# A gated cross-attention and expert block: input norm and attention in one part, context first

## The chip, the cores and the metric

The kernel runs on one NeuronCore of a Trainium2 chip. The engines are TensorE (PE; its weight loads are shown as PEld), VectorE (DVE), ScalarE (ACT), GpSimd (POOL) and the queue of SyncE (SP), which starts the DMAs. Each engine works through its own list of instructions in order and waits on semaphores. The metric is the device time of one execution in microseconds; lower is better.

## The reference

`x` is 8 sequences of 112 tokens with 512 channels (896 tokens), the context 8 sequences of 375 rows. The part around the change is this, cut to what matters:

```python
ln_out = _ln(hidden_states, ln_w, ln_b)          # hidden_states is a layer norm of x
q  = _ln(fp8_linear(ln_out, wq,  q_in_scale))    # 16 heads of 128
qx = _ln(fp8_linear(ln_out, wqx, qx_in_scale))
k  = _ln(fp8_linear(ln_out, wk,  k_in_scale))    # 8 groups
v  = fp8_linear(ln_out, wv, v_in_scale)
core = _gqa(q, k, v)
kx, vx = jnp.split(cond @ w_kv_x.T, 2, axis=-1)
xout = _gqa(qx, _ln(kx), vx)
catq = _div_clamp_fp8(concatenate([core, xout]), proj_smooth)
out  = catq @ wproj.T * (proj_in_scale * proj_w_scale)
```

`fp8_linear` divides its input by a scale, clips it to 448, rounds it to eight-bit floating point and multiplies it with the weights. The result goes through a tanh gate, is added to x, and a second part follows with another norm and eight experts of which each token takes two. That second part is not touched.

## The kernel before, in words

The kernel is written for five engines with every wait by hand. It has three parts, each a block of its own.

`quantise_inputs` (lines 231 to 400) is the input norm. The 896 tokens lie as TJ = 7 tiles of 128 in `xs`. Each tile is normed twice, one norm behind the other (the list NORMS, lines 238 to 244): DVE's bn_stats and bn_aggr (373, 363 to 366), GpSimd's power and product (303, 305), ACT's scaling in place (314). PE turns the tiles (347), ACT copies them with the norm's weight and bias into `hT` (320) and scales them once for each of the four projections into `yq` (330). DVE rounds each of the four, 3584 columns at a time, with five operations that wait for one another (`round_fp8`, 410 to 414), into `xq`. Between these, the weights of the first group (4 blocks k of 128 x 2048) are centred per head: DVE takes the means (130, 133), ACT applies them (149 to 154).

`attention` (472 to 1205) goes over 4 groups of heads, and in each over 8 sequences. `passes` (543 to 555) gives the order for all engines: first a step for (0,0) that only projects, then `step(s, t, ...)` in which the projections of s and the attention of t, the one before it, are interleaved. A position s = (g, u) with u < 7 has a tile of tokens. The six projections of a position (`project`, 852 to 877) are: 0 queries, 1 cross queries, 2 keys and values, 3 to 5 the three chunks of the context. They use the two banks of `p_proj` in turn, so that `project` j waits until ACT's `take` (709) of j - 2 is done. Their weights exist as a high and a low part (`w_hi` by ACT, 684; `w_lo` by DVE or GpSimd, 567), as does the context (`c_hi` by ACT, 689; `c_lo` by GpSimd, 638). Before a position's first projection DVE casts its tile of `xq` (`inputs`, 1043 to 1050).

In a step DVE's list is: `sums(s, 0)`, `max_self`, `max_cross` 0 and 1, `norm_self` (1080), `norm_cross` 0 and 1 (1093), `take_self` (1099), and so on, then `smoothed` 0 and 1 (1111) with `inputs` of the next position between them, in the first four steps of a group `weights.means` for the next group, and the rounding of the results (`results.exponents`, `results.rounded`, 196 to 215). PE's list (979 to 1010) has `project(s, 3)` between the scores and `turn_self` (926), which needs norm_self. For the first position, `first`, ACT makes all of w_hi, then c_hi, then takes 0 to 5 (823 to 829); DVE makes w_lo of three pieces (1190 to 1202) and GpSimd of two (647 to 649).

SP loads x, the small vectors and the weights in `quantise_inputs` (279 to 289) and the context of the first sequences in `attention`.

`projected_experts` (from 1212) is the output projection and the experts.

Of the kernel before, what the change touches and what calls it, by code (L numbers as in the profile page):

```python
# [19 lines left out]
U16 = mybir.dt.uint16  # L20
# [40 lines left out]
def transformer_block(nc, x, ctxT, vecs, scalars, smooth, w_in, wproj, Wr, Wg, Wu, Wd, out):  # L61
# [3 lines left out]
    with ExitStack() as top:  # L65
# [24 lines left out]
        with ExitStack() as c:  # L90
            xq = sb(c, "xq", [P, 4, KB, NT], BF16)
            smi = sb(c, "smi", [P, GP, 8])
            wsc = sb(c, "wsc", [P, 4, KB])
            wmul = sb(c, "wmul", [P, KB, LNC // HD])
            weights = CentredWeights(c, sb, sem, w_in, shared, wsc, wmul)
            with ExitStack() as c0:
                quantise_inputs(nc, c0, sb, ps, sem, x, vecs, scalars, smooth, vec, scal, gate,
                                proj_scale, ident, mhalf, epst, xq, smi, weights)
            with ExitStack() as c1:
                attention(nc, c1, sb, ps, sem, ctxT, wproj, cat_w, vec, ident, mhalf, epst, xq, smi,  # L100
                          weights, shared, wp_load, cat_load, results)
# [5 lines left out]
class CentredWeights:  # L107
# [3 lines left out]
    def __init__(self, c, sb, sem, w_in, shared, wsc, wmul):  # L111
# [3 lines left out]
        self.in_done = sem(c, "w_in_done")  # L115
# [115 lines left out]
def quantise_inputs(nc, c, sb, ps, sem, x, vecs, scalars, smooth, vec, scal, gate, proj_scale,  # L231
                    ident, mhalf, epst, xq, smi, weights):
# [11 lines left out]
    N = len(NORMS)  # L244
    wsc, wmul = weights.wsc, weights.wmul

    xs = sb(c, "xs", [P, TJ, D])
    st = sb(c, "st", [P, N, 6])
    mv = sb(c, "mv", [P, N, 2])
    rstd = sb(c, "rstd", [P, N])  # L250
    shift = sb(c, "shift0", [P, N])
    hT = sb(c, "hT", [P, KB, NT])
    inv = sb(c, "inv", [P, 4, KB])
    smr = sb(c, "smr", [P, GP, 8])
    yq = sb(c, "yq", [P, 2, KB, NT], BF16)
    ye = sb(c, "ye", [P, KB, NT], BF16)
    ysum = sb(c, "ysum", [P, KB, NT], BF16)
    pt = ps(c, "pt", [P, 4, 512])

    vec_in = sem(c, "vec_in")  # L260
    x_in = [sem(c, f"x_in{j}") for j in range(TJ)]
    const_done = sem(c, "const_done")
    pool_self = sem(c, "pool_self")
    bn_done = sem(c, "bn_done0")
    ag_done = sem(c, "ag_done0")
    stat_done = sem(c, "stat_done")
    rstd_pow = sem(c, "rstd_pow0")
# [1699 lines left out]
```

## Time and profile before

| | us |
|---|---|
| median of 3 runs | 1180.48 (1179.2 to 1185.28) |
| the profiled execution | 1179.41 |
| its span | 1177.6 |
| PE busy | 1081.8 (92% of the span) |
| DVE busy | 808.2 (69%) |
| ACT busy | 726.1 (62%) |
| GpSimd busy | 500.3 (42%) |

The span runs from the first to the last recorded instruction; the profiled execution's time is 1.8 us longer. Busy times are averages over the whole program and say nothing of one stage. In the rows further down, a timeline row gives the start and the duration in us, the engine, the line of the kernel, the operation, out<-in with the shapes, and in brackets how long the engine had been idle and what ended that. In rows of groups the numbers behind the bar are the busy time in us and the mean duration of one in ns. PEclk is the clock granted to TensorE as a share of its full 2.4 GHz.

### The profile page before, as it was taken

The page shows a single profiled execution, that of the slowest core. Times are in us where ns is not written, and L with a number is a line of the kernel's source. Part 1 is how long each engine was busy: PE and PEld are TensorE (multiplying, and loading weights), DVE is VectorE, ACT ScalarE, POOL GpSimd, SP SyncE. Part 2 cuts the span into 40 slices and gives each one's busy share as a digit, 9 for nine tenths or more (in the row PEclk, how much of TensorE's full clock was granted, in tenths as well). Part 3 has the DMA queues.
Part 4 walks back from the last instruction along what each step waited for, and adds up shares of the span by engine and source line. Part 5 has one row for each costly group of instructions (what it writes and reads, how often), then busy time and mean ns, then how long its engine had stood idle before and what let it go on. Part 6 is the DMA issues. An engine that isn't in the chain of part 4 may idle for free. (4 is left out here: it accounts for less than half of the span.)

```text
span 1177.6 us, 19559 instructions
## 1 busy us (share of the span) xinstructions
PE 1081.8 (92%) x5662; PEld 890.0 (76%) x5662; DVE 808.2 (69%) x1626; ACT 726.1 (62%) x2082; POOL 500.3 (42%) x587
## 2 busy tenths in 40 slices
PE   1079999999999999999999999998999959999996
PEld 1058888878888887888878888886888747777885
DVE  7967887797878787878789677767545776565000
ACT  7967887865788876687875676565231323333442
POOL 3065454445454544554545445542000125565432
PEclk9589999999999999999999999999999969999999
DMA  5032111115111113211111411110955237674220
GB/s 206 0 135 104 43 44 35 36 60 186 35 51 44 44 35 137 101 44 35 51 52 36 140 52 37 42 43 10 342 187 194 104 129 217 193 228 120 49 45 0
DMA packets 51714, 107.38 MB, mean 91 GB/s; under 512 B 5984, under 2 KB 26464, under 8 KB 49568
## 3 DMA queue, kind: packets, MB, share of 16 engines
q1 hardware_dynamic: 46912, 97.00, 25.2%
q0 software_dynamic: 4704, 9.18, 3.4%
q8 instruction: 49, 0.80, 0.3%
q14 instruction: 49, 0.40, 0.1%
HBM read 91.48 MB, written 16.52 MB: 92 GB/s over the span
## 5 line engine op out<-in xcount | busy, mean ns | idle before, releaser
L632 POOL TENSOR_TENSOR rs<-va,mhalf 125x2 f32<-125x2 f32 (+1 forms) x180 | 201.3, 1118 | 14.1
L638 POOL TENSOR_TENSOR c_lo<-c_raw,c_hi 128x500 fp32r<-128x500 f32 x96 | 122.8, 1279 | 183.3 <-ACT c_hi L689 183.3
L848 PE MATMUL p_proj<-w_hi,xqs 128*128 128x512 f32 (+2 forms) x464 | 157.0, 358 | 42.8 <-DVE w_lo L567 41.0
L875 PE MATMUL p_proj<-w_hi,c_hi 128*125 128x512 f32 x384 | 165.4, 431 | 0.0
L875 PE MATMUL p_proj<-w_hi,c_lo 128*125 128x512 f32 x384 | 151.5, 395 | 0.0
L875 PE MATMUL p_proj<-w_lo,c_hi 128*125 128x512 f32 x384 | 151.3, 394 | 0.0
L848 PE MATMUL p_proj<-w_lo,xqs 128*128 128x512 f32 (+2 forms) x464 | 147.9, 339 | 0.0
L848 PEld LDWEIGHTS p_proj<-w_hi,xqs 128*128 128x128 f32 (+1 forms) x464 | 86.4, 186 | 51.4 <-issue 43.5
L625 POOL TENSOR_TENSOR va<-ss,epst 125x2 f32<-125x2 f32 (+1 forms) x180 | 47.2, 262 | 170.7 <-DVE ss L1057 101.1
L767 ACT ACTIVATE pcross<-p_cross,nmax 112x375 f32<-112x375 f32 x128 | 73.6, 585 | 43.5 <-DVE nmax L1086 43.4
L919 PE MATMUL p_cross<-kxT,qxT 128*112 128x375 f32 x256 | 97.0, 480 | 0.0
L848 PEld LDWEIGHTS p_proj<-w_lo,xqs 128*128 128x128 f32 (+1 forms) x464 | 86.7, 187 | 8.3
L875 PEld LDWEIGHTS p_proj<-w_hi,c_hi 128*125 128x125 f32 x384 | 71.3, 186 | 18.4 <-issue 0.2
L875 PEld LDWEIGHTS p_proj<-w_lo,c_hi 128*125 128x125 f32 x384 | 71.3, 186 | 17.9
L875 PEld LDWEIGHTS p_proj<-w_hi,c_lo 128*125 128x125 f32 x384 | 71.1, 185 | 18.0
L729 ACT ACTIVATE nkx<-p_proj 125x256 f32<-125x256 f32 x96 | 38.4, 400 | 63.5 <-PE p_proj L875 63.5
L950 PE MATMUL p_out<-pcrossT,valx 125*128 125x224 f32 x354 | 76.6, 352 | 0.0
L1093 DVE TENSOR_SCALAR pcross<-pcross,linv 112x375 f32<-112x375 f32 x128 | 72.0, 562 | 4.6
L1086 DVE TENSOR_REDUCE nmax<-p_cross 112x1 f32<-112x375 f32 x128 | 69.0, 543 | 2.9 <-PE p_cross L919 0.2
L1469 POOL DMA_INDIRECT out<-p_cat,of_row x21 | 45.9, 2186 | 57.9 <-ACT p_cat L1570 50.2
L950 PEld LDWEIGHTS p_out<-pcrossT,valx 125*128 125x128 f32 x354 | 66.8, 189 | 0.3
L933 PEld LDWEIGHTS p_tr<-ident,pcross 112*125 112x125 f32 x384 | 51.9, 188 | 17.7 <-issue 13.5
(268 smaller groups left out, 2857.1 us busy)
## 6 DMA issues: line engine op xcount, KB each, us to landing
c_raw<-in_ctxT SPq DMA_DIRECT2D x96, 250.0 KB, 2.6
shared<-in_w_in SPq DMA_DIRECT2D x16, 1024.0 KB, 8.9
shared<-in_wproj SPq DMA_DIRECT2D x32, 256.0 KB, 3.9
raw_g<-in_Wg SPq DMA_DIRECT2D x8, 1024.0 KB
raw_u<-in_Wu SPq DMA_DIRECT2D x8, 1024.0 KB, 6.2
raw_d<-in_Wd SPq DMA_DIRECT2D x8, 1024.0 KB, 5.5
cat_scratch<-results SPq DMA_DIRECT2D x32, 224.0 KB, 2.0
shared<-cat_scratch SPq DMA_DIRECT2D x2, 1792.0 KB, 9.2
```

What stands on the lines that cost most here:

```text
L625: pool.tensor_tensor(va[0:rows, lo:hi], ss[0:rows, lo:hi], epst[0:rows, lo:hi], ALU.add).then_inc(va_done, 1)
L632: pool.tensor_tensor(rs[0:rows, lo:hi], va[0:rows, lo:hi], mhalf[0:rows, lo:hi], ALU.pow).then_inc(rs_done, 1)
L638: pool.tensor_tensor(flat(c_lo[:, k, :, :]), flat(c_raw[:, k, :, :]), flat(c_hi[:, k, :, :]).bitcast(F32), ALU.subtract).then_inc(cl_done, 1)
L767: act.activation(pcross[0:T, h, :], p_cross[0:T, h % 2, 0:TC], ACT.Exp, bias=nmax[0:T, 4 + h:5 + h], accum_out=lsum[0:T, 4 + h:5 + h]).the ...
L848: m = pe.matmul(out, xqs[:, n, k, 0:rows], (w_hi, w_lo)[i % 2][:, k, lo:lo + w], start=(i == 0), stop=(i == 2 * KB - 1))
L875: m = pe.matmul(bank[0:CT, :], a[:, ch, k, :], w[:, k, CKX:CV], start=(i == 0), stop=(i == 3 * KB - 1))
L919: pe.matmul(p_cross[0:T, h % 2, 0:TC], qxT[:, t[1] % 2, h, :], kxT[:, h // HPG, :], start=True, stop=True).then_inc(sx_rdy, 1)
L933: m = pe.transpose(p_tr[0:CT, 1 - h % 2, k * T:(k + 1) * T], pcross[0:T, h, k * CT:(k + 1) * CT], ident[0:T, 0:T])
L950: m = pe.matmul(out[:, HPG * T:2 * HPG * T], valx[0:CT, par, k, g * P:(g + 1) * P], flat(pcrossT[0:CT, k, HPG * g:HPG * (g + 1), :]), star ...
L1086: v.tensor_reduce(nmax[0:T, 4 + h:5 + h], p_cross[0:T, h % 2, 0:TC], AX, ALU.max, negate=True).then_inc(mx_done, 1)
L1093: v.tensor_scalar(pcross[0:T, h, :], pcross[0:T, h, :], linv[0:T, 4 + h:5 + h], None, ALU.mult).then_inc(nx_done, 1)
L1469: pool.indirect_dma_start(out=tokens[:, :], out_offset=bass.IndirectOffsetOnAxis(ap=of_row[:, 1, i:i + 1], axis=0), in_=y[:, i % 2, :], in ...
```

## The change

- `quantise_inputs` is gone as a block of its own. Its work is at the start of each engine's list in `attention`. `xs` shares its memory with `pcross`, `valx` and `pcrossT`, and the turned tiles `pt` are the eight banks of PSUM that attention uses.
- One norm instead of two: the variance is scaled by 1 + EPS and EPS squared is added. The norm's weight and bias go into the scale and offset (`xsc`, `xof`) with which ACT writes `xq` straight from PSUM, four activations of 896 columns per block k (`scaled_inputs`).
- The context's weight columns are loaded, centred and split first, the context's three chunks ahead of the other weights. PE's first position projects in the order 3, 4, 5, 0, 1, 2 (`turn_of` changes the semaphore numbers accordingly).
- The means and the centring of the first group's other weights go to DVE (k = 1 to 3) and GpSimd (k = 0) (`own_means`, `own_columns`); all four w_lo pieces of it are DVE's.
- The rounding is done per tile of 128 tokens, in two halves of two blocks k each, in place in `xq` (`rounding`): tile 0 before the first `inputs`, tiles 1 and 2 in the first position's work, tile s[1] + 2 at the end of DVE's list in the steps (0,1) to (0,4) (`spread`).
- `sqx` has one buffer in place of three, and ACT waits for its preceding take before it squares.

```diff
-    LAG = 3
-    NORMS = []
-    for j in range(TJ + LAG):
-        if j < TJ:
-            NORMS.append((0, j))
-        if j >= LAG:
-            NORMS.append((1, j - LAG))
...
-        for n in range(4):
-            v.wait_ge(y_done, n + 1)
-            round_fp8(v, link, flat(xq[:, n, :, :]), flat(yq[:, n % 2, :, :]), flat(ye[:, :, :]),
-                      flat(ysum[:, :, :])).then_inc(round_done, 1)
...
+    def own_columns(eng, k):
+
+        eng.wait_ge(weights.mu, k + 1)
+        for h in range(CKX // HD):
+            cols = w_raw[:, k, h * HD:(h + 1) * HD]
+            n = 0 if h < CQX // HD else 1 if h < CK // HD else 2
+            eng.tensor_scalar(cols, cols, weights.wsc[:, n, k:k + 1], weights.mean[:, k, h:h + 1], ALU.mult, ALU.add)
+        cols = w_raw[:, k, CV:WC]
+        eng.tensor_scalar(cols, cols, weights.wsc[:, 3, k:k + 1], None, ALU.mult).then_inc(w_cen, 1)
...
+        sp.dma_start(w_raw[:, :, CKX:CV], weights.w_in[0, :, :, CKX:CV]).then_inc(wx_in, 16)
+        for k in range(NC):
+            load_c(0, 0, k)
+        for k in range(KB):
+            sp.dma_start(w_raw[:, k, 0:CKX], weights.w_in[0, :, k, 0:CKX]).then_inc(weights.in_done[k], 16)
+            sp.dma_start(w_raw[:, k, CV:WC], weights.w_in[0, :, k, CV:WC]).then_inc(weights.in_done[k], 16)
...
         def step(s, t, g, change, k):
-            if change == "first":
-                w_low(g, 2)
-                w_low(g, 3)
             if s is None:
                 return
-            if has_tile(s):
+            if change == "first":
+                for j in range(3):
+                    c_low(s, j)
+                own_columns(pool, 0)
+                for j in (3, 4, 5, 0, 1, 2):
+                    rstd(s, j)
+            elif has_tile(s):
...
         def summed_squares(s, j):
 
             act.wait_ge(va_done, st_no(before(s), j))
+            act.wait_ge(pj_done, pj_no(s, j) - 1)
...
+        def scaled_inputs(k):
+
+            for n in range(4):
+                last = act.activation(xq[:, n, k, :], pt[:, k, 0:NT], ACT.Identity, bias=xof[:, n, k:k + 1],
+                                      scale=xsc[:, n, k:k + 1])
+            last.then_inc(y_done, 1)
...
             if change == "first":
-                for n in range(len(USED)):
+                scaled_inputs(0)
+                w_high(g, 4, change)
+                for j in range(3):
+                    c_high(s, j)
+                for j in range(3):
+                    scaled_inputs(j + 1)
+                    take(s, j + 3)
+                for n in range(4):
                     w_high(g, n, change)
                 for j in range(3):
-                    c_high(s, j)
-                for j in range(6):
                     take(s, j)
...
+            if change == "first":
+                for j in (3, 4, 5, 0, 1, 2):
+                    project(s, j, g)
+                return
...
+        def rounding(u, half, first, last):
+
+            y = xq[:, :, 2 * half:2 * half + 2, u * P:(u + 1) * P]
+            e = re[:, :, :, :]
+            v.wait_ge(y_done, 2 * half + 2)
+            for n in range(first, last + 1):
+                v.wait_ge(rq, 10 * u + 5 * half + n)
+                if n == 0:
+                    ins = v.tensor_scalar(y, y, FP8_MAX, -FP8_MAX, ALU.min, ALU.max)
+                elif n == 1:
+                    ins = v.tensor_scalar(e.bitcast(U16), y.bitcast(U16), 0x7F80, None, ALU.bitwise_and)
+                elif n == 2:
+                    ins = v.tensor_scalar(e, e, 2.0 ** -6, 1.5 * 2.0 ** 4, ALU.max, ALU.mult)
+                else:
+                    ins = v.tensor_tensor(y, y, e, (ALU.add, ALU.subtract)[n - 3])
+                ins.then_inc(rq, 1)
...
+            spread = s is not None and s[0] == 0 and 1 <= s[1] < TJ - 2
...
             if Q and A and change != "queries": results.rounded(v, lin(t))
+            if spread:
+                rounding(s[1] + 2, 0, 0, 4)
+                rounding(s[1] + 2, 1, 0, 4)
             if change == "new": smooth_of(g)
             if change == "first":
-                w_low(g, 0)
-                w_low(g, 1)
                 w_low(g, 4)
+                for j in range(1, KB):
+                    own_means(j)
+                for j in range(1, KB):
+                    own_columns(v, j)
+                rounding(0, 0, 0, 4)
+                rounding(0, 1, 0, 4)
+                inputs(s)
+                for n in range(4):
+                    w_low(g, n)
                 smooth_of(g)
-                for j in range(6):
-                    if j < 3:
-                        sums(s, j)
-                    if j > 0:
-                        scale(s, j - 1)
-                    if j == 3:
-                        inputs((s[0], s[1] + 1))
-                scale(s, 5)
-
-        inputs(FIRST)
+                for j in range(3, 6):
+                    scale(s, j)
+                rounding(1, 0, 0, 4)
+                rounding(1, 1, 0, 4)
+                for j in range(3):
+                    sums(s, j)
+                inputs((s[0], s[1] + 1))
+                for j in range(3):
+                    scale(s, j)
+                rounding(2, 0, 0, 4)
+                rounding(2, 1, 0, 4)
+
+        for j in range(TJ):
+            statistics(j)
+        scales_of_inputs()
+        other_columns()
+        constants()
+        own_means(0)
         passes(v, step)
```

## Rows read from the trace of the kernel before

**Rows 1.** The page's PE line over 40 equal slices of the span.

```profile
PE   1079999999999999999999999998999959999996
```

**Rows 2.** By stage: us; PE, PEld, DVE, ACT, POOL busy; PEclk; DMA.

```profile
0.00:60.00 60.00, 5.56 (x28) 4.74 (x28) 51.38 (x100) 52.14 (x92) 11.13 (x36) 0.71 0.27 101
107.13:130.96 23.83, 23.83 (x134) 19.95 (x133) 19.06 (x42) 19.62 (x65) 11.81 (x15) 1.00 0.15 43
```

**Rows 3.** PE timeline, first matmul of step (0,1).

```profile
83.39 0.47 PE L848 MATMUL p_proj<-w_hi,xqs 128*128 128x512 f32 x1
```

**Rows 4.** Step (0,2), timeline of DVE and PE, with idle time before.

```profile
115.32 0.62 DVE L1072 TENSOR_REDUCE nmax<-p_self 112x4 f32<-112x448 f32 x1 [1.58 <-PE p_self L912]
...
117.67 0.62 DVE L1080 TENSOR_TENSOR pself<-pself,linv 112x448 f32<-112x448 f32 x1
...
119.50 0.55 PE L926 MATMUL p_tr<-ident,pself 112*112 112x112 f32 x4
...
120.08 0.62 DVE L1099 COPY pselfT<-p_tr 112x448 f32<-112x448 f32 x1 [0.73 <-PE p_tr L926]
...
131.34 0.62 DVE L1111 TENSOR_TENSOR results<-p_out,smg 128x448 bf16<-128x448 f32 x1 [1.11 <-PE p_out L950]
```

**Rows 5.** Norm of the tokens, 0 to 25 us: groups and one start.

```profile
L373 DVE BATCH_NORM_STATS2 st<-xs x14: 683/684/695, 3.6 to 16.9; 128x6 f32<-128x512 f32 x14
L314 ACT ACTIVATE xs<-xs,shift,rstd x14: 812/814/815, 7.7 to 19.7; 128x512 f32<-128x512 f32 x14
L303 POOL TENSOR_TENSOR rstd<-mv,mhalf 128x1 f32<-128x1 f32 x14 | 7.7, 551 | 6.5 <-DVE mv L366 5.3
5.68 0.69 DVE L373 BATCH_NORM_STATS2 st<-xs 128x6 f32<-128x512 f32 x1 [1.37 <-DMA xs<-in_x]
```

**Rows 6.** ACT timeline: start, us for all, instructions.

```profile
20.38 5.01 ACT L320 ACTIVATE hT<-pt,vec 128x512 f32<-128x512 f32 x8
60.40 7.41 ACT L684 ACTIVATE w_hi<-shared 128x2048 fp32r<-128x2048 f32 x5 [0.62 <-PEq L96]
67.71 1.62 ACT L689 ACTIVATE c_hi<-c_raw 128x500 fp32r<-128x500 f32 x3
```

**Rows 7.** DVE timeline, then groups by shape (busy us, mean ns).

```profile
20.46 1.75 DVE L130 TENSOR_REDUCE w_mean<-shared 128x12 f32<-128x1536 f32 x1 [0.17 <-DVE proj_scale L394]
60.73 1.10 DVE L1049 CAST xqs<-xq 128x512 fp32r<-128x512 bf16 x3 [1.83 <-PEq L835]
62.34 4.49 DVE L567 TENSOR_TENSOR w_lo<-shared,w_hi 128x2048 fp32r<-128x2048 f32 x2 [0.21 <-ACT w_hi L684]
L410 DVE TENSOR_SCALAR yq<-yq 128x3584 bf16<-128x3584 bf16 x4 | 4.3, 1088 | 1.1 <-ACT yq L330 1.1
L413 DVE TENSOR_TENSOR ysum<-yq,ye 128x3584 bf16<-128x3584 bf16 x4 | 8.1, 2026 | 0.1
L202 DVE TENSOR_SCALAR results<-results 128x896 bf16<-128x896 bf16 x32 | 12.5, 389 | 0.0
L212 DVE TENSOR_TENSOR results<-results 128x896 bf16<-128x896 bf16 x32 | 19.9, 623 | 0.9
```

**Rows 8.** DVE beside GpSimd and alone, timeline; then a GpSimd group.

```profile
99.78 1.27 POOL L638 TENSOR_TENSOR c_lo<-c_raw,c_hi 128x500 fp32r<-128x500 f32 x1
...
100.25 1.02 DVE L1093 TENSOR_SCALAR pcross<-pcross,linv 112x375 f32<-112x375 f32 x1
...
101.37 0.42 DVE L1093 TENSOR_SCALAR pcross<-pcross,linv 112x375 f32<-112x375 f32 x1
...
L1440 POOL TENSOR_SCALAR minus<-ident 128x128 fp32r<-128x128 f32 x1 | 0.7, 721 | 0.0
```

**Rows 9.** PE idle and its clock: timeline, then a stretch by engine.

```profile
813.11 0.59 PE L926 MATMUL p_tr<-ident,pself 112*112 112x112 f32 x4 [1.81 <-DVE pself L1080]
...
823.34 0.47 PE L1598 MATMUL p_acc<-hi_g,hi_d 128*128 128x512 f32 x1 [2.43 <-DVE lo_g L1770]
...
823.68:827.00 3.32, 3.32 (x10) 2.57 (x9) 3.18 (x7) 0.40 (x1) 2.96 (x6) 0.52 1.03 366
```

More of the change, by code:

```diff
@@ L95, in transformer_block @@
             weights = CentredWeights(c, sb, sem, w_in, shared, wsc, wmul)
[L96 to L101, printed above, removed]
+            attention(nc, c, sb, ps, sem, x, vecs, scalars, smooth, ctxT, wproj, cat_w, vec, scal, gate,
+                      proj_scale, ident, mhalf, epst, xq, smi, weights, shared, wp_load, cat_load, results)
         with ExitStack() as c:
@@ L114, in __init__ @@
         self.mean = sb(c, "w_mean", [P, KB, LNC // HD])
-        self.in_done = sem(c, "w_in_done")
+        self.in_done = [sem(c, f"w_in_done{k}") for k in range(KB)]
         self.seen = sem(c, "w_seen")
@@ L469, with attention @@
 FIRST = (0, 0)
-def attention(nc, c, sb, ps, sem, ctxT, wproj, catd, vec, ident, mhalf, epst, xq, smi,
-              weights, shared, wp_load, cat_load, results):
+def attention(nc, c, sb, ps, sem, x, vecs, scalars, smooth, ctxT, wproj, catd, vec, scal, gate,
+              proj_scale, ident, mhalf, epst, xq, smi, weights, shared, wp_load, cat_load, results):
     w_raw, w_cen = weights.raw, weights.cen
@@ L681, in w_high @@
                 act.wait_ge(pj_rdy, pj_no((g - 1, u), j))
-            act.wait_ge(w_cen, 4 * (g + 2))
+            if change == "first" and n == 4:
+                act.wait_ge(wx_cen, 1)
+            else:
+                act.wait_ge(w_cen, 4 * (g + 2))
             lo, hi = USED[n]
@@ L857, in project @@
                 pe.wait_ge(xqs_done, lin(s) + 1)
+            if s == FIRST and j == 3:
+                pe.wait_ge(y_done, 1)
             if j < 2:
@@ L1010, in step @@
             if Q: outputs(t, 1)
+        pe.wait_ge(const_done, 1)
+        for j in range(TJ):
+            pe.wait_ge(normed, j + 1)
+            for k in range(KB):
+                m = pe.transpose(pt[:, k, j * P:(j + 1) * P], xs[:, j, k * P:(k + 1) * P], ident[:, :])
+            m.then_inc(tr_done, 1)
         passes(pe, step)
@@ new lines, in other_columns @@
+        def other_columns():
+            heads = w_raw[:, :, CKX:CKX + 2 * HD].rearrange("p k (h d) -> p k h d", d=HD)
+            mean = weights.mean[:, :, CKX // HD:CKX // HD + 2]
+            v.wait_ge(wx_in, 16)
+            link(v.tensor_reduce(mean, heads, AX, ALU.add))
+            link(v.tensor_scalar(mean, mean, -1.0 / HD, None, ALU.mult))
+            for k in range(KB):
+                for h in range(CKX // HD, CKX // HD + 2):
+                    cols = w_raw[:, k, h * HD:(h + 1) * HD]
+                    last = v.tensor_scalar(cols, cols, weights.mean[:, k, h:h + 1], None, ALU.add)
+            last.then_inc(wx_cen, 1)
```

297 lines of the change are left out of this document (130 added, 167 removed).

## The prediction

> **What bounds the kernel now.** I read first the page's line of TensorE over the span: it is idle in the first two of 40 slices, full from then on [rows 1]. The table by stage says how: in the first 60 us, the input norm with its rounding and the centring of the first weights, PE works 5.56 us while DVE and ACT work 51 and 52 us each; in a step of attention PE is busy 23.83 of 23.83 us and DVE 19.06 [rows 2]. So there are two regimes. Up to the start of step (0,1), at 83.39 us [rows 3], the time is the chain through ACT and DVE; afterwards it is PE, and DVE has under 4.8 us to spare per step. The timeline of a step tells where that spare time lies [rows 4]: DVE waits 1.58 us for the self scores (it reaches max_self early), 0.73 us for the turned probabilities and 1.11 us for the last output. PE has slack of its own: DVE ends norm_self at 117.67 + 0.62 = 118.29 and PE turns the result at 119.50, 1.2 us later. The change shortens the first regime and puts work in DVE's spare time of the second.
>
> **The head, part by part.** One norm instead of two: six tiles follow the second, which starts at 5.68 us; bn_stats takes 0.68 and the aggregate and two scalings behind it, now waited for one by one, some 0.38 (estimate): 5.68 + 6 × 1.07 = 12.1. GpSimd's power 0.55 and product, ACT's 0.81 and four transposes bring tr_done to 14.8 us [rows 5].
>
> scaled_inputs: 16 activations of 896 columns from PSUM. ACT's price comes out of three rows [rows 6]: 1.62 us for three of 500 and 7.41 for five with 8192 columns give 0.83 ns per column and 0.13 us fixed; eight of 448 on average with bias and scale take 5.01, which is 0.63 each, so 0.26 fixed; 896 columns cost 1.0, and four of them 4.0 us. The first four end at 18.8; w_hi of the context's columns (1.87) at 20.7, three c_hi at 22.3. DVE by then has centred these columns (one reduction and eight short operations after 12.9) and waits; its w_lo takes 4.49/2 = 2.25 us [rows 7] and ends at 23.0. GpSimd's c_lo (1.27) [rows 8] comes behind it, so PE starts project 3 at 24.4 instead of after everything. It runs at half clock, 5.0 us, to 29.4. ACT: take 3 to 30.7, scaled_inputs(2) to 34.7, take 4 to 35.9, scaled_inputs(3) to 39.9, take 5 to 41.2, the first own w_hi to 43.1.
>
> DVE meanwhile: three own_means at 1.75 × 1280/1536 + 0.2 = 1.7, to 28.1. own_columns for three k: 33 operations, 30 of them 128 wide. None is in the trace. The nearest is 0.42 us for 375 columns [rows 8]; taking off what a short one costs anyway (0.39 at 896 against 1.09 at 3584 leaves 0.16 [rows 7]) I get 0.25, and 0.2 from start to start. That makes 6.8 us; bounds 5 and, at 0.42 each, 14. They end at 34.9, with collisions (below) at 37. The rounding of half a tile is five operations on 1024 columns. Rows of 3584 and of 896 give 0.26 ns per column for the three with scalars and 0.52 for the two of two tensors [rows 7]: 3 × 0.46 + 2 × 0.73 = 2.84 us, 5.7 a tile. The second half of tile 0 needs y_done 4 (39.9) and ends at 43.2. From there DVE alone carries the head: inputs 1.4, four w_lo 6.8, three scales and smooth_of 1.2, rounding of tile 1 5.7, sums 1.6, inputs 1.4: 61.3 us. GpSimd's w_low of two pieces is gone, DVE has them.
>
> Collisions: beside a c_lo (99.78 to 101.05) DVE's normalisation took 1.02 us, alone 0.42 [rows 8]. GpSimd now runs three c_lo and own_columns(0) beside DVE; 11 operations at 0.3 to 0.72 (the row of its own 128x128 scalar operation). I take 1.7 us that reach the end, bounds 0 and 6. So step (0,1) starts at 63.0 against 83.39; PE, idle for some 7 us before, starts it at half clock and loses about 1.9 us on the first project and turns. **Gain of the head 83.4 − 63.0 − 1.9 = 18.5 us**, between 14 and 20.
>
> At nothing I put: SP's changed order (all four weight blocks had landed by 20.46 us [rows 7]; now 0.75 MB of context goes ahead, and the last block is read after 26 us, so some 3 us of delay are free; if not, own_means moves and has 3 us before y_done 4); own_columns on GpSimd before its rstd (those results are read after 52 us); the one sqx buffer (ACT waits on its own previous take, long past); the parts merged into one (the change of block lies within the 83.39); take 2's squares now wait for sums 0, which DVE reaches at 58.7, and sums 2 comes right behind it.
>
> **The steps.** Tile 2 is rounded while PE does the first projections of (0,1): DVE arrives at max_self within 1 us of PE, price 0. Tiles 3 to 6 are rounded at the end of steps (0,1) to (0,4), 5.7 us in one stretch between the rounding of the results and sums 0. Behind it on DVE queue sums 0 and max_self; for max_self wait exp_self on ACT with takes 2 and 3 behind it, then norm_self, then PE's turn_self; GpSimd's rstd 0 and c_lo 1 wait for sums 0. What is late: 5.7 − 1.58 − 1.2 = 2.9 us of PE idle, between project 3 and turn_self. DVE gets its 0.73 back, and PE then waits for take_self, some 0.3 us; ACT's c_high 0 at that time releases a c_lo that collides with the rounding, 0 to 0.9 us (rows 8 show 0.6). The wait of 1.11 us before smoothed(1) shows that DVE has caught up by the end, so nothing accumulates and nothing is regained. 3.5 us a step, bounds 2.9 and 4.2: **loss of 4 × 3.5 = 14.0 us**. The slack of these four is the same: each has weights.means.
>
> **TensorE's clock.** After 2.43 us of idle time PE ran the next 3.3 us at 0.52, that is at 1.2 GHz; after 1.81 us its four transposes took 0.59, as without a wait (0.55) [rows 4, 9], at 2.4 GHz. Idle times of 3.5 us lie beyond both. A stretch like that of 3.3 us costs 1.6 us. As an estimate between never and always I take two of four steps: **3.2 us**, bounds 0 and 6.4. The Trainium skill, TensorE: Matmul & The Clock Gate, section HAM oscillation, describes a kernel that re-throttles between bursts again and again; by that reading all four steps pay, 3.2 us more than my sum. The row at 823.34 agrees with it, that at 813.11 does not.
>
> **Sum.** −18.5 + 14.0 + 3.2 = −1.3. The profiled execution took 1179.41 us (span 1177.6); the median of the runs is 1180.48, 1.07 above. From 1178.1, with half of that added, I say 1178.6 us: no change that can be measured, since about 0.5% (5.9 us) is what a measurement of this kernel can tell.
>
> **Rivals.**
> (a) The collisions stay out and the clock holds: step (0,1) starts at 61.3, gain 20.2; the steps cost 3.1 each, 12.4. 1179.4 − 7.8 + 0.5 = 1172. For it: a wait of 1.81 us left the clock up. Against: 3.1 is more than 2.43.
> (b) The clock falls in all four, and the columns on GpSimd and DVE block each other one by one, 3 us in the head: 1178.6 + 3.2 + 3 = 1185. For it: 1.02 against 0.42. The Trainium skill, SBUF — State Buffer, section Who interferes with whom, calls the pair of ports a lock, held for a whole instruction; the row with 1.02 us agrees.
> (c) Slower. DVE's rounding on slices: y is four times two pieces of 128 columns with strides, while the rows of before are of one unbroken stretch. If the short pieces make the scalar operations run like those of two tensors (0.73 in place of 0.46) and those at twice that (1.3), half a tile takes 4.8 us, a tile 9.6. The head has two roundings in its chain (1.5 tiles), each step one: 5.5 × 3.9 = 21 us more, 1200 us. It decides from 7.1 us a tile on, where the change is slower by over 0.5%. Against: casts of xqs, also four pieces of 128, take 1.10 us for three [rows 7], no more than their columns ask for.
> (d) The roundings vanish in DVE's idle time, or the head is all that counts: 1179.4 − 18.5 = 1161. Against it stands the order of the queue: 5.7 us in one piece against 1.58 and 1.2.
>
> That the change does not do what it says would be a rounding off the DVE or a head still serial; the diff leaves no room for it, and I count it under (d).
>
> **Chances.** Forecast 0.45, with its own range of 1174 to 1184; (a) 0.22; (b) 0.17; (c) 0.10; (d) 0.06. Under 1174.6: nearly all of (a), (d), and a little of the forecast, 0.32. Over 1186.4: (c) and some of (b), 0.14. Between, 0.54. The range of 1168 to 1187 leaves out (c), (d) and the ends of (a) and (b).
>
> **What the profile would show.** Right: y_done 1 near 19 us, project 3 near 24, project 0 near 47, step (0,1) at 61 to 65; roundings of 2.8 us per half; steps (0,2) to (0,5) some 3.5 us longer in PE, with idle time before turn_self released by norm_self, none before max_self on DVE; later groups as before. Wrong: step (0,1) before 59 or after 67 us, PE waiting at another place than turn_self (project 3 for c_lo, or project 4 for take 2), a half of the rounding over 3.2 us, the clock at half in every step or in none, or later groups of other length.

## The result and the profile after

| | before | after |
|---|---|---|
| median of 20 runs each, on the same chips (us) | 1180.87 (1179.09 to 1185.28) | 1184.37 (1182.78 to 1186.43) |
| the profiled execution | 1179.41 | 1182.78 |
| its span | 1177.6 | 1180.6 |
| PE / DVE / ACT / GpSimd busy | 1081.8 / 808.2 / 726.1 / 500.3 | 1094.9 / 820.3 / 698.8 / 490.6 |

The ratio is 1.0028, 95% interval 1.002 to 1.0036: 3.5 us slower, outside what chance would give, and less than 0.5%. The profiled execution of after is the fastest of its 20. Its granted clock over the whole span was 0.966, that of twelve others 0.963; 0.003 of 1182 us is some 3.5 us of missing clock more in those (an estimate from these two numbers; where they lose it isn't on record). The accounts below are of the profiled one. Every run counted here and below is a fast one but one of e3_eight_of_ten, 1393.28 us at a granted clock of 0.742, which its ratio leaves out.

The page's lines of TensorE, after (busy tenths in 40 slices, then the granted clock):

```profile
PE   4498888999999999999999999998999959999996
PEclk8789988999999999999999999999999969999999
```

Against [rows 1] two things are new. The first two slices are no longer nearly empty: PE works while the inputs are made. And slices 4 to 7 (88 to 206 us), all 9 before, are 8, two of them with a clock of 8 tenths. That is nearly the whole story: an earlier start, paid back in four steps.

The timeline of after, 0 to 65 us, by engine:

```profile
24.51 0.76 PE L789 MATMUL bank<-w_hi,c_hi 128*125 128x512 f32 x1 [9.54 <-POOL c_lo L527]
47.52 0.77 PE L760 MATMUL bank<-w_hi,xqs 128*128 128x512 f32 x1 [12.68 <-DVE w_lo L432]
61.52 0.77 PE L760 MATMUL bank<-w_hi,xqs 128*128 128x512 f32 x1 [5.97 <-DVE xqs L1061]
...
28.95 3.39 DVE L426 TENSOR_SCALAR shared<-shared,wsc,w_mean 128x128 f32<-128x128 f32 x10
32.40 2.64 DVE L426 TENSOR_SCALAR shared<-shared,wsc,w_mean 128x128 f32<-128x128 f32 x10
38.05 0.41 DVE L1043 TENSOR_SCALAR xq<-xq 128x1024 bf16<-128x1024 bf16 x1
39.42 1.42 DVE L1049 TENSOR_TENSOR xq<-xq,re 128x1024 bf16<-128x1024 bf16 x2
45.09 6.76 DVE L432 TENSOR_TENSOR w_lo<-shared,w_hi 128x2048 fp32r<-128x2048 f32 x4
...
26.79 4.55 POOL L426 TENSOR_SCALAR shared<-shared,wsc,w_mean 128x128 f32<-128x128 f32 x10
```

The first row is project 3 (24.4 forecast), the second project 0 (near 47), the third the first matmul of step (0,1), at 61.52 (63.0 forecast) against 83.39 [rows 3]. A column operation of 128 elements comes every 0.26 us, and every 0.34 beside GpSimd's own ten; a half of the rounding is 0.41 + 0.43 + 0.43 + 1.42 us and some gaps, 2.9.

From there I follow one mark, the first matmul of `score_self` in each step (L912 before, L826 after). It comes 19.86 us earlier in step (0,1) (70.65 against 90.51), still 19.84 in (0,2), then 14.35, 8.55 and 1.91 earlier, and in (0,6) 4.84 **later** (214.54 against 209.70). It stays 4.7 to 4.9 us later until the output projection. So the four intervals that hold a rounding at their start lose 24.7 us. The mark of (0,6), before and after:

```profile
209.70 0.95 PE L912 MATMUL p_self<-kT,qT 128*112 128x112 f32 x8
214.54 0.95 PE L826 MATMUL bank<-kT,qT 128*112 128x112 f32 x8
```

The timeline of the first of the four intervals, after, answers to [rows 4]:

```profile
93.21 0.42 DVE L1043 TENSOR_SCALAR xq<-xq 128x1024 bf16<-128x1024 bf16 x1
94.58 2.35 DVE L1049 TENSOR_TENSOR xq<-xq,re 128x1024 bf16<-128x1024 bf16 x2
98.43 1.42 DVE L1049 TENSOR_TENSOR xq<-xq,re 128x1024 bf16<-128x1024 bf16 x2
99.77 0.68 DVE L1068 TENSOR_REDUCE ss<-sq 128x4 f32<-128x512 f32 x1
100.36 0.61 DVE L1083 TENSOR_REDUCE nmax<-bank 112x4 f32<-112x448 f32 x1
102.71 0.79 DVE L1091 TENSOR_TENSOR pself<-pself,linv 112x448 f32<-112x448 f32 x1
...
94.15 1.50 POOL L527 TENSOR_TENSOR c_lo<-c_raw,c_hi 128x500 fp32r<-128x500 f32 x1 [5.79 <-ACT c_hi L580]
...
101.01 0.35 ACT L651 ACTIVATE pself<-bank,nmax 112x112 f32<-112x112 f32 x1 [4.90 <-DVE nmax L1083]
...
103.55 1.00 PE L840 MATMUL bank<-ident,pself 112*112 112x112 f32 x4 [3.74 <-DVE pself L1091]
132.87 0.60 PE L840 MATMUL bank<-ident,pself 112*112 112x112 f32 x4 [3.72 <-DVE pself L1091]
162.54 0.99 PE L840 MATMUL bank<-ident,pself 112*112 112x112 f32 x4 [3.74 <-DVE pself L1091]
193.02 0.99 PE L840 MATMUL bank<-ident,pself 112*112 112x112 f32 x4 [3.72 <-DVE pself L1091]
```

Read it down: DVE rounds from 93.21 to 99.8; the pair of additions beside GpSimd's `c_lo` takes 2.35 us, the one without it 1.42. Behind it come sums 0 and max_self, with no bracket, since the scores have long been there; ACT has waited 4.90 us for that maximum; norm_self ends at 103.5, and PE, with nothing to do in between, has been idle for 3.74 us. The idle time is the same in all four steps: 14.9 us. Yet the transposes take 1.00 us in place of 0.55 in three of them. The table by stretch says why (us; busy time of PE, PEld, DVE, ACT, POOL; PEclk; DMA share and GB/s):

```profile
103.55:107.05 3.50, 3.50 (x13) 2.83 (x14) 3.10 (x9) 2.98 (x12) 1.09 (x2) 0.53 0.29 78
132.87:138.40 5.53, 5.40 (x20) 3.74 (x21) 5.16 (x14) 4.32 (x17) 3.26 (x3) 0.69 0.18 49
162.54:168.60 6.06, 6.06 (x19) 4.47 (x19) 5.32 (x14) 4.30 (x17) 3.02 (x5) 0.52 0.18 42
193.02:199.10 6.08, 6.08 (x18) 4.51 (x19) 5.35 (x14) 4.32 (x17) 3.04 (x5) 0.51 0.16 42
828.07:831.39 3.32, 3.32 (x15) 2.73 (x16) 3.18 (x7) 0.74 (x2) 3.23 (x8) 1.00 0.94 310
```

Behind each of the four idle times PE works at 1.2 GHz, for some 3.4 us behind the first two and 6 us behind the others. Busy time times the missing clock is 1.6, 1.7, 2.9 and 3.0: 9.2 us, with the 14.9 nearly all of the 24.7. The last row gives something back: where [rows 9] had 0.52 after an idle time of 2.43 us, after has 1.00 behind one of 2.42, and the output projection is 1.6 us shorter. The account of the span: −19.9 + 24.7 − 1.6 = +3.2, measured 3.0.

The trace also tells the short falls from the long ones. This is the clock in the last microsecond of the second and of the third idle time, with PE still idle:

```profile
131.87:132.87 1.00, 0.00 (x0) 0.00 (x1) 0.97 (x3) 1.00 (x5) 0.46 (x1) 1.00 0.00 0
161.54:162.54 1.00, 0.00 (x0) 0.00 (x0) 0.97 (x3) 1.00 (x5) 0.47 (x1) 0.50 0.00 0
```

In the third the clock was down before PE started again, and PE then ran slowly for 6 us; in the second it fell later, and PE ran slowly for 3.4.

### The profile page after: what moved, and what is told of

The parts are those of the page before. It is cut to its first block and busy times, and to the rows that moved or that the text cites. A ratio compares the mean times of both kernels' runs of the same rounds, so it can differ in the third digit from the quotient of the medians.

```text
span 1180.6 us, 19656 instructions
## 1 busy us (share of the span) xinstructions
PE 1094.9 (93%) x5662; PEld 898.1 (76%) x5662; DVE 820.3 (69%) x1695; ACT 698.8 (59%) x2015; POOL 490.6 (42%) x582
## 5 line engine op out<-in xcount | busy, mean ns | idle before, releaser
L789 PE MATMUL bank<-w_hi,c_hi 128*125 128x512 f32 x384 | 167.8, 437 | 9.5 <-POOL c_lo L527 9.5
L760 PE MATMUL bank<-w_hi,xqs 128*128 128x512 f32 (+2 forms) x464 | 158.0, 360 | 18.7 <-DVE w_lo L432 12.7
L789 PE MATMUL bank<-w_hi,c_lo 128*125 128x512 f32 x384 | 152.4, 397 | 0.0
L789 PE MATMUL bank<-w_lo,c_hi 128*125 128x512 f32 x384 | 152.4, 397 | 0.0
L760 PE MATMUL bank<-w_lo,xqs 128*128 128x512 f32 (+2 forms) x464 | 148.8, 341 | 0.0
L760 PEld LDWEIGHTS bank<-w_hi,xqs 128*128 128x128 f32 (+1 forms) x464 | 87.0, 187 | 27.3 <-issue 19.2
L833 PE MATMUL bank<-kxT,qxT 128*112 128x375 f32 x256 | 101.4, 499 | 0.0
L659 ACT ACTIVATE work<-bank,nmax 112x375 f32<-112x375 f32 x128 | 73.6, 585 | 43.1 <-DVE nmax L1097 43.0
L760 PEld LDWEIGHTS bank<-w_lo,xqs 128*128 128x128 f32 (+1 forms) x464 | 87.2, 188 | 8.4
L789 PEld LDWEIGHTS bank<-w_lo,c_hi 128*125 128x125 f32 x384 | 72.2, 188 | 18.5 <-issue 0.9
L864 PE MATMUL bank<-work 125*128 125x224 f32 x384 | 83.1, 352 | 0.0
```

What stands on the lines that cost most here:

```text
L659: act.activation(pcross[0:T, h, :], p_cross[0:T, h % 2, 0:TC], ACT.Exp, bias=nmax[0:T, 4 + h:5 + h], accum_out=lsum[0:T, 4 + h:5 + h]).the ...
L760: m = pe.matmul(out, xqs[:, n, k, 0:rows], (w_hi, w_lo)[i % 2][:, k, lo:lo + w], start=(i == 0), stop=(i == 2 * KB - 1))
L789: m = pe.matmul(bank[0:CT, :], a[:, ch, k, :], w[:, k, CKX:CV], start=(i == 0), stop=(i == 3 * KB - 1))
L833: pe.matmul(p_cross[0:T, h % 2, 0:TC], qxT[:, t[1] % 2, h, :], kxT[:, h // HPG, :], start=True, stop=True).then_inc(sx_rdy, 1)
L864: m = pe.matmul(out[:, HPG * T:2 * HPG * T], valx[0:CT, par, k, g * P:(g + 1) * P], flat(pcrossT[0:CT, k, HPG * g:HPG * (g + 1), :]), star ...
```

## The experiments

The twelve kernels stand here as edits of `step` in DVE's list, unless said otherwise; they are edits of the kernel after, and e12 alone of the kernel before. A ratio is to runs of the kernel before on the same chip, whose medians were 1180.5 to 1180.9; each new kernel ran 4 to 10 times. All differences from before are under 2%. "Intervals" are the four between the marks of (0,2) and (0,6), as excess over 23.85 us. Medians are of all runs; idle times and intervals are of the one profiled execution of each.

| kernel | median us | ratio to before (95%) | idle of PE before turn_self | excess of the four intervals |
|---|---|---|---|---|
| after | 1184.37 | 1.0028 (1.002–1.0036) | 3.74 3.72 3.74 3.72 | 5.49 5.80 6.64 6.72 |
| e1_no_lumps | 1160.2 | 0.9824 (0.9802–0.9846) | none | 0 0 0 0 |
| e2_half_lumps | 1165.39 | 0.9871 (0.9852–0.9891) | 0.84 0.84 0.84 0.85 | 1.30 1.31 1.26 1.32 |
| e3_eight_of_ten | 1176.79 | 0.9970 (0.9959–0.9981) | 2.28 2.30 2.26 2.29 | 4.35 3.93 2.68 4.03 |
| e4_pe_kept_busy | 1177.0 | 0.9963 (0.9947–0.9978) | 0.58 0.58 0.59 0.58 | 4.19 4.17 4.20 4.20 |
| e5_two_places | 1175.78 | 0.9954 (0.9938–0.9969) | 2.33 1.62 1.62 1.57 | 4.39 3.73 3.75 3.66 |
| e6_four_places | 1168.97 | 0.9895 (0.9878–0.9912) | 0.92 1.20 1.15 0.92 | 1.67 2.00 3.57 1.69 |
| e7_low_on_gpsimd | 1185.44 | 1.0043 (1.0027–1.006) | 3.74 3.72 3.72 3.71 | 6.91 6.92 6.89 6.89 |
| e8_no_tile_one | 1180.71 | 1.0000 (0.999–1.0009) | 3.75 3.74 3.72 3.72 | 6.77 6.82 6.81 6.84 |
| e9_both | 1167.91 | 0.9901 (0.9883–0.992) | 0.92 1.15 1.17 1.17 | 1.73 1.95 1.97 1.93 |
| e10_two_blocks | 1166.83 | 0.9888 (0.9872–0.9905) | 0.92 1.21 1.13 1.17 | 1.67 2.02 1.91 1.92 |
| e11_block_on_gpsimd | 1166.8 | 0.9875 (0.9852–0.9898) | 0.92 1.17 1.19 1.20 | 1.72 1.94 1.95 1.96 |
| e12_before_with_lumps | 1204.56 | 1.0196 (1.0172–1.0221) | 4.18 4.20 4.20 4.18 | 6.28 6.62 6.73 6.77 |

### How much the rounding in the steps costs

```diff
             if spread:
-                rounding(s[1] + 2, 0, 0, 4)
-                rounding(s[1] + 2, 1, 0, 4)
+                v.sem_inc(rq, 10)
```

That is e1. `v.sem_inc` only advances the counter on which the operations wait for one another. In e2 the first line stays and `v.sem_inc(rq, 5)` takes the place of the second; in e3 the second is `rounding(s[1] + 2, 1, 0, 2)` with `v.sem_inc(rq, 2)`. What isn't rounded there is left out.

> The changed kernel without the rounding of tiles 3 to 6 (their inputs stay unrounded; all else is as in the changed kernel). Theory, slack and clock: the four steps behind the roundings took 5.5, 5.8, 6.6 and 6.8 us more than before, 24.7 in all, and the head gave 19.9. Without the roundings the steps are 23.85 us again and the time is 1184.4 - 24.7 = 1160, or 1161 to 1162 if the stage behind attention is longer again as in the kernel before. Rival, DVE in proportion: the same. Rival, the head paid part of it: then the steps keep some of their length and the time stays above 1165.

> The changed kernel with only the first half (blocks 0 and 1) of the rounding of tiles 3 to 6, 2.84 us a step; the other half is left out. Theory, slack and clock: DVE has 1.6 us before max_self and PE 1.2 us before turn_self, together 2.8, so the half costs 0 to 1 us a step (1 where a c_lo of GpSimd collides) and the clock stays: 0 to 4 us above the kernel without these roundings. Rival, DVE in proportion to its work: half of 24.7, so 12 us above it.

> The changed kernel with eight of the ten operations of each rounding of tiles 3 to 6; the last addition and subtraction of the second half (1.46 us) are left out. Theory, slack and clock: PE's idle time before turn_self falls from 3.73 to some 2.3 us a step, 9 us in all above the kernel without these roundings; with the clock at half after it 15 to 18, without it 9 to 11. The case asks from what idle time on the clock falls; 1.81 us left it up, 3.73 did not. Rival, DVE in proportion: 0.74 of 24.7, 18 us.

Without the rounding (e1) the time is 1160.2 and no interval is longer than before: the head is worth some 20 us, and the four roundings cost 24.2. Half a rounding (e2) costs 5.2, not 12, and not nothing: there is slack, but 2.9 us already exceed it by 0.84 at turn_self. Eight of ten operations (e3) cost 16.6. So the cost grows faster than the work. Below are the timeline of e3 and the table by stretch, 6 us behind each of its four idle times:

```profile
101.60 0.60 PE L840 MATMUL bank<-ident,pself 112*112 112x112 f32 x4 [2.28 <-DVE pself L1091]
...
157.57 0.59 PE L840 MATMUL bank<-ident,pself 112*112 112x112 f32 x4 [2.26 <-DVE pself L1091]
```

```profile
101.60:107.60 6.00, 5.87 (x22) 4.31 (x23) 5.44 (x16) 4.57 (x17) 3.42 (x5) 0.72 0.14 43
129.82:135.82 6.00, 6.00 (x24) 4.64 (x25) 5.53 (x16) 4.63 (x18) 3.36 (x5) 0.74 0.17 45
157.57:163.57 6.00, 5.88 (x29) 4.52 (x30) 5.86 (x15) 5.15 (x19) 3.67 (x4) 1.00 0.18 45
184.12:190.12 6.00, 6.00 (x23) 4.70 (x24) 5.53 (x16) 4.63 (x18) 3.37 (x5) 0.72 0.17 45
```

The four idle times are alike within 0.04 us; the clock fell behind three of them and held behind the third, and that interval is the shorter one, 2.68 against 3.93 to 4.35. The difference, 1.3 to 1.7 us, is the price of one fall at its smaller size.

### Is it the clock, or the idle time alone?

```diff
             if A: project(s, 3, g)
+            if A and s[0] == 0 and 2 <= s[1] <= 5:
+                pe.wait_ge(ya_done, 2 * (lin(t) + 1))
+                for i in range(14):
+                    pe.matmul(p_out[:, :], w_hi[:, i % KB, 0:P], w_hi[:, i % KB, CKX:CV], start=True, stop=True)
             if Q: turn_self(t)
```

An edit of PE's list. It adds work whose result nobody reads.

> The changed kernel, nothing left out; in steps (0,2) to (0,5) PE runs 14 extra matmuls of 512 columns (3.3 us) into the free bank p_out behind project 3, where it would be idle for 3.73 us. Theory, slack and clock: the wait for norm_self stays, 14.9 us in all, but the clock stays at 2.4 GHz, and the other 9.8 us go: 1174 to 1177. Rival, the 9.8 us are contention on DVE and GpSimd and not the clock: 1184 as before, or more.

The timeline of e4 and its stretch:

```profile
100.41 3.33 PE L921 MATMUL bank<-w_hi 128*128 128x512 f32 x14
104.33 0.60 PE L840 MATMUL bank<-ident,pself 112*112 112x112 f32 x4 [0.58 <-DVE pself L1095]
```

```profile
104.33:110.33 6.00, 5.90 (x29) 4.52 (x30) 5.86 (x15) 5.11 (x18) 3.67 (x4) 1.00 0.19 45
```

PE waits just as long for norm_self, but fills the wait, and behind it the clock is 1.00 in all four steps. Useless work makes the kernel 7.4 us **faster** than after (1177.0 against 1184.37). Idle time and falling clock are two terms, and e4 takes away only the second. It also prices the first: with the clock held, an interval is still 4.2 us longer, 3.7 of it at turn_self and some 0.45 behind it, 16.7 us in four; the clock is then the other 7.9 of the 24.7.

### The same work in more places

e5 puts the first half behind `inputs`, ahead of `scale(s, 3)`, and leaves the second at the end. e6 cuts it in four; all the rounding is done:

```diff
+            late = s is not None and s[0] == 0 and 2 <= s[1] < TJ - 1
...
             if Q: norm_cross(t, 1)
+            if late:
+                rounding(s[1] + 1, 1, 2, 2)
             if Q: take_self(t)
...
             if A: scale(s, 1)
+            if late:
+                rounding(s[1] + 1, 1, 3, 4)
             if A: scale(s, 2)
...
             if A: inputs((s[0], s[1] + 1))
+            if spread:
+                rounding(s[1] + 2, 0, 0, 1)
             if A: scale(s, 3)
...
             if spread:
-                rounding(s[1] + 2, 0, 0, 4)
-                rounding(s[1] + 2, 1, 0, 4)
+                rounding(s[1] + 2, 0, 2, 4)
+                rounding(s[1] + 2, 1, 0, 1)
```

> The changed kernel, nothing left out; the rounding of tiles 3 to 6 is split in place: the first half behind inputs, the second where both stood. Theory, slack and clock: behind inputs DVE waits 1.1 us for the last output, so the first half makes it 1.7 us late; with the second half behind it, less 2.8, PE waits 1.8 us a step before turn_self, 2.7 where a c_lo collides. That is 7 to 11 us above the kernel without these roundings if the clock holds, 1168 to 1172, and 6 to 10 more if it falls. Rival, DVE in proportion to its work: as much as in one go, 1184.

> The changed kernel, nothing left out; the ten operations of each rounding of tiles 3 to 6 stand in four places where DVE waits: two behind inputs, five at the end of the step, one before take_self of the next step and two before its scale 2. Theory, slack and clock: DVE's work of a step is 24.8 us against PE's 23.85, so at least 0.9 us a step stays, with collisions up to 1.8, and no idle time of PE is long enough for the clock: 4 to 8 us above the kernel without these roundings, 1164 to 1169. Rival, DVE in proportion to its work: 1184.

The timeline of e6 and its stretches:

```profile
126.65 0.59 PE L840 MATMUL bank<-ident,pself 112*112 112x112 f32 x4 [1.20 <-DVE pself L1091]
...
152.45 0.60 PE L840 MATMUL bank<-ident,pself 112*112 112x112 f32 x4 [1.15 <-DVE pself L1091]
```

```profile
126.65:132.65 6.00, 5.77 (x28) 4.18 (x29) 5.89 (x15) 4.79 (x17) 3.40 (x4) 1.00 0.15 43
152.45:158.45 6.00, 5.78 (x20) 3.97 (x21) 5.89 (x15) 4.79 (x18) 3.40 (x4) 0.72 0.18 45
```

e6 is 15.4 us faster than after and 1.05% faster than before, with the same instructions. Two places (e5) give 8.6: its idle times of 1.6 us still drop the clock each time. In e6 it fell once, behind 1.15 us, and not behind 1.20. What is left in e6, 1.7 to 2.0 us a step, is hardly a matter of place any more: from 88 to 118 us its DVE rows show one idle time of the step, 0.60 us before the reciprocal at 99.76, so DVE itself is the bound there. [rows 2] told half of it: 23.83 − 19.06 = 4.8 us free against 5.7 of work.

### Does the head play a part in the loss?

e12 leaves the kernel before as it is and adds one stretch of DVE work at the same place; what is rounded again are values rounded already:

```diff
             if Q and A and change != "queries": results.rounded(v, lin(t))
+            if s is not None and s[0] == 0 and 1 <= s[1] < TJ - 2:
+                again(s[1] + 2)
...
```

> The kernel before, with nothing of the change but one stretch of 5.8 us more on DVE at the end of the steps (0,1) to (0,4): the values of the fourth to seventh tile, rounded already, are rounded once more in place (104 of 128 columns a piece, ten operations, and three clips more to make up for the width). Theory (the steps lose by themselves, whatever the head does): each of the four steps becomes longer by 3.7 us of TensorE idle before turn_self and by 1.7 to 3.1 us of half clock behind it, 5.5 to 6.9, and the time is 1180.5 + 22 to 27 = 1205. Rival (the loss comes from the new head: SP's other order, the shared memory of the tokens, the takes in another order): the steps stay at 23.85 us or lose the 2.9 us of the prediction alone, 1181 to 1192.

Timeline of e12:

```profile
124.24 0.59 PE L928 MATMUL p_tr<-ident,pself 112*112 112x112 f32 x4 [4.18 <-DVE pself L1082]
...
154.39 0.99 PE L928 MATMUL p_tr<-ident,pself 112*112 112x112 f32 x4 [4.20 <-DVE pself L1082]
```

23.8 us slower than before, with nothing of the new head in it. The loss belongs to the stretch alone. (The idle time is 4.2 us here and not 3.7; why isn't traced.)

### The head

e7 gives two of DVE's four low parts back to GpSimd, as before had them:

```diff
                 own_columns(pool, 0)
-                for j in (3, 4, 5, 0, 1, 2):
+                for j in (3, 4, 5):
                     rstd(s, j)
+                for n in (2, 3):
+                    pool.wait_ge(wh_done[n], g + 1)
+                    split_low(pool, n).then_inc(wl_done[n], 1)
+                for j in range(3):
+                    rstd(s, j)
...
-                for n in range(4):
+                for n in range(2):
                     w_low(g, n)
```

> The changed kernel with two of the first group's four own low parts (pieces 2 and 3) made by GpSimd again, behind its rstd of the context, where it is idle from 41.9 to 59.2 us; everything else stays. Theory (the head's end is DVE's chain, TensorE idles 5.97 us before step (0,1)): DVE has 3.4 us less to do; the next bound is TensorE's project 2, which needs GpSimd's two pieces (44.6 + 2 x 4.2 = 53 us), then its take and sums 2. So step (0,1) starts 2.5 us earlier than at 61.5, at 59.0, and the time is 2 to 3 us under the changed kernel's 1184.4: 1182. Rival (the two engines block each other): GpSimd's 8.4 us beside DVE's casts and rounding, whose operations wait for whole operations of GpSimd, give the 3.4 us back or more: step (0,1) at 61.5 to 64, time 1184 to 1187.

> The changed kernel without the rounding of the second tile (ten operations, 5.7 us, in DVE's list behind the scales of the context; that tile's values stay unrounded, left out). Theory: the chain of the head runs through it, but only down to the next bound, which is close: TensorE ends project 2 at 55.5 us, ACT's squares follow to 56.7, sums 2 and inputs to 58.5. So step (0,1) starts 3.0 us earlier, not 5.7, at 58.5, and the time is 3 us under the changed kernel's: 1181.4. Rival (DVE alone carries the head to its end, as the prediction had it): 5.7 us, step (0,1) at 55.8, 1178.7. Third: another chain (the context's rstd, the weights) already ends there: no gain.

Timeline of e7:

```profile
45.51 8.11 POOL L432 TENSOR_TENSOR w_lo<-shared,w_hi 128x1024 fp32r<-128x1024 f32 x2 [3.52 <-ACT w_hi L580]
...
44.70 6.67 DVE L432 TENSOR_TENSOR w_lo<-shared,w_hi 128x2048 fp32r<-128x2048 f32 x2
51.30 2.35 DVE L956 COPY smg<-smi 128x8 f32<-128x8 f32 x1
...
63.23 0.77 PE L765 MATMUL bank<-w_hi,xqs 128*128 128x512 f32 x1 [5.34 <-DVE xqs L1066]
```

The rival won in the trace. DVE's two parts take as long as its four did in after (6.76), and a copy of 8 columns takes 2.35 us: it ends at 53.65, when GpSimd's second part does (53.62). In after it is this row:

```profile
51.77 0.16 DVE L951 COPY smg<-smi 128x8 f32<-128x8 f32 x1
```

Step (0,1) starts 1.7 us later. In time e7 and after can't be told apart (1.0043 and 1.0028, with intervals that overlap); that the gain of 2 to 3 us did not come is clear. e8 leaves out `rounding(1, ...)` in the first position (that tile stays unrounded), and 5.8 us of work off DVE bring step (0,1) only 3.4 us forward, as the theory had it (3.0):

```profile
54.53 0.69 DVE L1068 TENSOR_REDUCE ss<-sq 128x4 f32<-128x512 f32 x1 [0.48 <-ACT sq L588]
56.26 0.42 DVE L1068 TENSOR_REDUCE ss<-sq 128x2 f32<-128x256 f32 x1 [1.05 <-ACT sq L588]
...
58.13 0.77 PE L760 MATMUL bank<-w_hi,xqs 128*128 128x512 f32 x1 [2.87 <-DVE xqs L1061]
```

DVE now waits for ACT's squares of PE's projections: the next bound of the head is some 3 us away. In both kernels every fall of the clock in the steps is of the long kind (in e8 the 6 us behind each idle time are at 0.50), and all intervals cost 6.8 to 6.9 us.

### The best version

e9 is e6 with e7's edit; e10 is e9 with `own_columns(pool, 1)` added and DVE's loop from 2; e11 is e6 with these two edits and all four low parts on DVE.

> The rounding of the fourth to seventh tile in four places (as in e6_four_places) and the two low parts on GpSimd (as in e7_low_on_gpsimd). Theory: the two are independent, the gains add: e6 had 1169.0, so 1166.5. Rival: GpSimd's work beside DVE takes the second gain back: 1169 to 1171.

> As e9_both, and GpSimd also scales the columns of a second block (k = 1) in place of DVE: 11 operations, 5.5 us on GpSimd, 3 us off DVE. Theory: DVE ends its columns at 35 in place of 38 us, but the second half of tile 0 waits for ACT's fourth block at 39.5 us, so 1.4 us are gained at most, and GpSimd's rstd of the context comes 5.5 us later, where only the scales behind the low parts ask for it: 1165 to 1166.5. Rival: TensorE's first own projection needs ACT's high parts (from 40.3 to 46.0 us) and does not start earlier, or GpSimd's longer list beside DVE costs what it saves: as e9_both or 1 to 2 us more.

> The changed kernel with the rounding in four places (e6_four_places, 1169.0 us) and the columns of block k = 1 scaled by GpSimd in place of DVE; all four own low parts stay with DVE. It takes from e10_two_blocks (1166.8) the part that was seen to cost: there the two low parts on GpSimd made DVE's two low parts take 6.67 us in place of 3.4 and a copy of 8 columns 2.35. Theory: DVE ends its columns 3 us earlier, waits 0.6 us for ACT's fourth block and gains 1.2 us in all; step (0,1) starts near 60.3, and the time is 1166.5 to 1168. Rival: the low parts on GpSimd were a gain after all, and without them the time goes back to e6's 1169 or above.

Timeline of e11:

```profile
39.34 0.53 DVE L1044 TENSOR_SCALAR xq<-xq 128x1024 bf16<-128x1024 bf16 x1 [0.55 <-ACT xq L666]
...
60.01 0.76 PE L761 MATMUL bank<-w_hi,xqs 128*128 128x512 f32 x1 [5.59 <-DVE xqs L1062]
```

In e11 DVE reaches ACT's fourth block 0.55 us early and step (0,1) starts at 60.01, 1.5 us earlier than after. e10 and e11 end at the same 1166.8, 1.1 to 1.25% under before and 17.6 us under after; e9 has e6's gain and no more: its step (0,1) starts at 63.74, later than after's, though its clock doesn't fall behind that step. There GpSimd's two parts met DVE's casts, 3.25 us for three in place of 1.10 in after:

```profile
43.97 3.25 DVE L1065 CAST xqs<-xq 128x512 fp32r<-128x512 bf16 x3
```

Between e9, e10, e11 and e6 the intervals overlap; that all four beat both kernels is clear, their order isn't. Part of what lies between them is the clock and not the edit: the profiled execution of e6 holds three falls behind (0,1), those of e9, e10 and e11 none up to 920 us.

## Why the prediction was wrong

The forecast was 1.3 us faster, no measurable change; measured are 3.5 slower. The range held the time, the sign didn't come out. By its own steps:

- **Head, −18.5 forecast, −19.9 measured.** Right in mechanism and nearly in size. The start of step (0,1) came at 61.52, not 63.0; the cold clock took the forecast 1.9 us (21.87 at the first matmul, 19.86 at score_self). Columns were 0.26 us each, not 0.2, and DVE ended tile 0 at 43.8, not 43.2; of the 1.7 us put down for collisions nothing more came behind that. DVE carries the head to its end, but the next bound lies only 3 us below (e8). One price had no row behind it: four low parts at 6.8 us, where [rows 7] gave 2.25 for one; measured were 6.76, so 1.69 each.
- **The rounding's own price, 2.84 a half:** 2.9. Rival (c), slow short pieces, is out: 0.43 and 0.71 us an operation against 0.46 and 0.73 forecast (the slopes of [rows 7] give 0.42 and 0.69, so the forecast had rounded up).
- **Idle time in the steps, 14.0:** 14.9 at turn_self alone, and 16.7 with all that e4 still loses while the clock holds, the upper bound of 4.2 a step. It stands where it was put, between project 3 and turn_self, with norm_self as the releaser, and nothing accumulates. The forecast's 2.9 of idle and a collision at the upper end of its 0 to 0.9 are the 3.73: the first pair of additions took 2.35 in place of 1.42 in all four. Tile 2 did cost nothing.
- **The clock, 3.2 taken, "bounds 0 and 6.4": this step failed.** Measured are 9.2 by the stretches and 7.9 by the intervals against e4 (where the clock is low, part of the 0.45 us behind turn_self may be hidden; that isn't shown). Two things in it were wrong. "As an estimate between never and always I take two of four steps": it was always, in after, e7, e8 and e12, behind 3.7 to 4.2 us, and the prediction's own list had "the clock at half in every step" among the signs of being wrong. And the bound itself: "a stretch like that of 3.3 us costs 1.6" took the one stretch seen in [rows 9] as the only size. The stretch also comes as one of 6 us, at 2.9 to 3.2. e4 shows the term by itself in the medians: 7.4 us with the clock held.
- **Rival (b)** named four falls, and 1185; the time is its, but half of its working isn't, since the 3 us of blocked columns did not come. The Trainium skill's section HAM oscillation (TensorE: Matmul & The Clock Gate), which the prediction set beside its sum, told which way the four steps would go; the trace agrees, and e3's third step (2.26 us) and three steps of e6 (0.92 to 1.20) show that with shorter idle times it can also not happen.
- **Not forecast:** the 1.6 us given back at the output projection. The same wait of 2.4 us met a clock that fell before and held after. Nothing in these runs ties that to the change: the wait stands in all fourteen kernels, and the clock fell behind it in six, with no order in which.

With four falls of the two sizes seen now, the prediction's own sum would have been −18.5 + 14.0 + 9.2 = +4.7. That the time still fell into the range was in part luck: the steps cost 7.5 us more than forecast (24.7 against 17.2), and the head and the output projection hid 3.0 of them.

## What to carry to other kernels

Before filling an engine's spare time, write down where it lies: DVE had 4.8 us free per step, but in pieces of 1.6, 0.7 and 1.1, and 5.7 us in one piece turned into 3.7 us of TensorE idle; in four pieces the same instructions cost 0.9 to 1.2. Count a new idle time of TensorE twice, as itself and as 1.6 to 3.2 us of half clock behind it: in these runs the clock fell every time behind 3.7 us, in half of the cases behind 1.6 to 2.4 us, and once in eleven behind 1.2. If the idle time can't be avoided, work of any kind for TensorE in it may pay (e4). Where the trace shows GpSimd's work making DVE's operations longer ([rows 8], e7), an idle GpSimd isn't spare for a path that runs through DVE: one block's columns moved there brought step (0,1) forward in e11, two long low parts put it back in e7.

## What the runs showed of the hardware

- Idle time and fall of the clock don't map one to one. Behind 0.58 to 0.92 us it held every time; of eleven idle times of 1.13 to 1.21 (e6, e9, e10, e11) it fell behind one, of 1.15. It fell behind 1.57 to 1.62 (e5), held behind 2.26 and fell behind 2.28 (e3). Two waits end attention in all fourteen kernels: behind the one of 1.81 us it fell in five (e2 to e6) and held in nine, behind the one of 2.42 or 2.43 it fell in six (before, e1, e2, e3, e5, e6) and held in eight. Behind 3.7 us and more it fell in all sixteen steps seen.
- PE worked at half clock for about 3.4 us or for about 6 behind idle times of the same 3.7 us, and for 3.4 and 4.7 to 5.2 behind the 4.2 us of e12; in e7 and e8, whose intervals are all alike, it was the long one each time (6.0 to 6.4 us). It goes with the moment of the fall: in all thirteen long ones the clock was down 0.4 to 2.1 us before PE started again, in the eleven short ones of these steps it fell between 0.3 us before that start and 2.1 us behind it. What sets that moment is not explained by these runs.
- DVE and GpSimd beside each other: two DVE low parts 6.67 us beside GpSimd's two (8.11), 3.4 alone (half of 6.76); a copy of 8 columns 2.35 against 0.16; three casts 3.25 against 1.10 (e9). The Trainium skill, SBUF — State Buffer, section Who interferes with whom, speaks of a lock held for a whole instruction; the trace agrees, with a short copy that ends within 0.03 us of GpSimd's instruction.
